# Query norms: in two columns the full high part of the Gram matrix times high parts of x only, read out times x and times the low part of x

## The chip, the cores and the metric

The kernel runs on one NeuronCore of a Trainium2 chip. The metric is the device time of one launch in microseconds. The kernel before takes 480.39 us (median of 3 runs, 479.73 to 480.58).

## What is computed

```
x1  = x + tanh(g0) * attend(layernorm(x), ctx)
      Q = layernorm(x) @ Wq.T + bq ;  K = rmsnorm(ctx) @ Wk.T + bk
      Q = rmsnorm(Q) * qn ;  K = rmsnorm(K) * kn
      attend = softmax(Q @ K.T / 32) @ rmsnorm(ctx)
out = x1 + tanh(g1) * (layernorm(x1) @ W_base.T + b_base + gated low-rank experts)
```

x is 4 batches of 512 tokens by 1024 features, ctx is 4 batches of 64 keys. All is float32. The scores need of Q only its product with K, which goes through a small matrix, and the norm of each of its rows. The norm is taken without forming Q: with z the scaled token and G = Wq^T Wq (rows centred), the square of the norm is z^T G z plus a bias term.

## The kernel before, in words

**High and low parts.** Each float32 operand of a matrix product is split into a high part (rounded to the fast format by ScalarE) and a low part (what is left, VectorE). A product of two such operands is three matmuls: high times high, low times high, high times low.

**Gram matrix.** The `g` stages fill it in two sweeps over banks of PSUM, as 36 blocks of 128x128, each pair (row, column) once, since it is symmetric. `g_out` evicts them: ScalarE writes the high part `gram[:, g, 0, :]`, VectorE the low part `gram[:, g, 1, :]` (L1196); blocks off the diagonal are scaled by 2, which stands for the mirrored block that is not kept. `k_norm` follows early in the second sweep. Then come eight `m` stages (L658 to L660), and then the loop over the four batches.

**Batch loop.** The order of all stages is one list written out by hand (`first`, then `last`), and each engine goes through it in that order and does its own part of each stage; nothing is reordered at run time. For batch b and column j = 0 to 7:

- `y` (b, j): TensorE sums over the blocks of column j, three matmuls each (L673 to L675), into one of three banks. Columns 0 to 7 have 1, 2, 3, 5, 5, 6, 7 and 7 blocks. VectorE's "dot" (L1340) reads the bank, adds a bias and multiplies by z: 128x512 into `sq`, of which there are two that alternate. GpSimd adds each `sq` to `sq_sum` (L1560). A dot waits until the sum has taken the `sq` two before; y (b, j) waits for the dot of three columns before.
- After y (b, 0): `tops` (L702, then L1354) of the batch before, and `mr`. After y (b, 1): `norms` (TensorE L694 adds `sq_sum` over partitions, VectorE L1348, GpSimd a root L1532), `fn_split` (VectorE L1380, two inputs in SBUF), `weights` (VectorE L1513, ScalarE four exponentials), all of the batch before.
- At j = 2: `z` (VectorE L1236) and `zh` (ScalarE) for the batch after, `shares` (VectorE L1360, L1366, L1367, L1369, which makes `px`) and `fn_low` (VectorE L1385) of the batch before. At j = 3: s, `scores`, and `pt`, the transposition of `px` (TensorE L516). In batches 0 and 1 most columns have an `x_stat` too (VectorE L1221, L1224).
- After y (b, 4) to y (b, 7) one `attend` each (TensorE L715, L716 in two halves, each in one of two banks; VectorE L1440 empties them). The next `attend` waits until the bank of its half is empty. It stands in VectorE's order behind `z`.
- In batch 3 VectorE has `stat` at j = 2 (L1160 on), the scaling of `bb` (L1447) at j = 3 and splits of the base weights (L1413) from j = 3 on.

After the loop come the heads and the base product, 8 pairs of token tiles (L736 to L778).

Of the kernel before, what the change touches and what calls it, by code (L numbers as in the profile page):

```python
# [5 lines left out]
P = 128  # L6
# [37 lines left out]
def build(nc, x, xt, ctx, ctxt, wq, wk, wb, hd, bt, vec, fn_w, b_base, scal, out):  # L44
# [9 lines left out]
    B = 4  # L54
# [15 lines left out]
    with ExitStack() as stack:  # L70
# [126 lines left out]
        a21 = at("a21", [P, KH, P], F32, r_a21)  # L197
        csum = at("csum", [P, S_ALL], F32, r_a21)
# [56 lines left out]

        def block_no(row, col):
            return BLOCKS.index((min(row, col), max(row, col)))
# [26 lines left out]
         v_xaggr, v_xvar, v_z, v_zl, v_wq, v_gl, v_ml, v_wb, v_dot, v_top, v_nb, v_rec, v_pxh, v_px, v_fnvar, v_fnw, v_fn,  # L284
         v_wt, v_wl, v_h3, v_hw, v_bb, v_bt, v_neg, v_s3, v_low, v_hg, v_nmax, v_g, v_mm, v_ev) = (
            sem(f"v_{n}") for n in ("ct", "ctxvar", "kw", "small", "stat", "aggr", "var", "kr", "kfull", "kt", "cs", "kb",
# [58 lines left out]
        for p in range(NP):  # L345
# [8 lines left out]
            for i, (n, z, *_) in enumerate(products(p)):  # L354
                if all(z != z_ for _, z_, *_ in products(p)[i + 1:]):
# [22 lines left out]
        for b in range(B):  # L378
            for j in range(FB):
# [23 lines left out]
                if b > 0:  # L403
                    first += {0: [("tops", b - 1)], 1: [("norms", b - 1), ("fn_split", b - 1), ("weights", b - 1)], 2: [("shares", b - 1), ("fn_low", b - 1)],
# [72 lines left out]
        def qsums(b, f):  # L477
            return b * (FB - 1) + f
# [26 lines left out]
        def tensor(pe):  # L505
# [27 lines left out]
            for stage, *i in stages:  # L533
# [90 lines left out]
                elif stage == "g":  # L624
                    sweep, f = i
                    blocks = [w[f][:, :].rearrange("p (c d) -> p c d", d=P) for w in (wqh, wql)]
                    for left, right in ((0, 0), (0, 1), (1, 0)):
                        if sweep == left == 0:
                            pe.wait_ge(*((v_wq, f + 1) if right else (a_wq, f + 1)))
                        for n_bank, pieces in SWEEPS[sweep]:  # L630
# [10 lines left out]
                            if f == FB - 1 and left == 1:  # L641
                                done.then_inc(p_g, 1)
                elif stage == "m":
# [5 lines left out]
                    if r < 2:  # L649
                        engine, count = ring.empty(r)  # L650
# [11 lines left out]
                elif stage == "y":  # L662
# [7 lines left out]
                    pe.wait_ge(v_zl, 4 * b + max(ROWS[j]) // CK + 1)  # L670
                    for r in ROWS[j]:
                        g = block_no(r, j)
                        pe.matmul(acc[:, :], gram[:, g, 0, :], xth[b % 2][:, r, :], start=r == ROWS[j][0], stop=False)  # L673
                        pe.matmul(acc[:, :], gram[:, g, 1, :], xth[b % 2][:, r, :], start=False, stop=False)  # L674
                        done = pe.matmul(acc[:, :], gram[:, g, 0, :], xtl[b % 2][:, r, :], start=False, stop=r == ROWS[j][-1])  # L675
# [13 lines left out]
                elif stage == "norms":  # L689
                    b, = i  # L690
                    acc = ring_open((stage, b), "dve")
                    pe.wait_ge(g_qsum, qsums(b, FB - 1))
# [48 lines left out]
                elif stage == "prod":  # L741
# [3 lines left out]
                    if opens and p == 0:  # L745
                        pe.wait_ge(*{"A": (v_dot, NQ - 2), "B": (v_dot, NQ - 1), "C": (v_first, 4), "D": (v_dot, NQ)}[n_bank])
# [34 lines left out]
        def sync(sp):  # L781
# [42 lines left out]
            for stage, *i in stages:  # L824
# [6 lines left out]
                elif stage == "load_xt":  # L831
# [7 lines left out]
                    else:  # L839
                        sp.wait_ge(p_y, nq(b - 2, FB - 1) + 1)  # L840
                        sp.wait_ge(v_dot, nq(b - 2, FB - 1) + 1)
# [22 lines left out]
                elif stage == "w_load":  # L864
                    op, = i
                    if op in ("B11", "B21", "B12"):
                        sp.wait_ge(p_y, nq(B - 2, FB - 1) + 1)
                        sp.wait_ge(v_dot, nq(B - 2, FB - 1) + 1)
                    elif op in ("B22", "T1", "T2", "T4"):
                        sp.wait_ge(p_y, NQ)  # L870
                        sp.wait_ge(v_dot, NQ)
# [65 lines left out]
        def scalar(act):  # L937
# [13 lines left out]
            for stage, *i in stages:  # L951
# [12 lines left out]
                elif stage == "rsb":  # L964
                    act.wait_ge(p_ring, ring.full((stage,)))
                    act.activation(rsb[:, :], bank[T_BANKS[ring.number[stage,] % 2]][:, 0:S_ALL], ACT.Copy).then_inc(ring_sem["act"], 1)
                elif stage == "tanh":
# [17 lines left out]
                elif stage == "g_out":  # L985
# [3 lines left out]
                    for n, (n_bank, pieces) in enumerate(SWEEPS[sweep]):  # L989
                        act.wait_ge(p_g, n + 1 + sweep * len(SWEEPS[0]))  # L990
                        for row, cols, off in pieces:
                            for c, col in enumerate(cols):
                                done = act.activation(gram[:, block_no(row, col), 0, :],
                                                      bank[n_bank][:, (off + c) * P:(off + c + 1) * P],
                                                      ACT.Copy, scale=1.0 if col == row else 2.0)
# [152 lines left out]
        def vector(dve):  # L1148
# [20 lines left out]
            for stage, *i in stages:  # L1169
# [19 lines left out]
                elif stage == "g_out":  # L1189
                    sweep, = i  # L1190
                    for n, (n_bank, pieces) in enumerate(SWEEPS[sweep]):
                        dve.wait_ge(a_gh, n + 1 + sweep * len(SWEEPS[0]))
                        for row, cols, off in pieces:
                            for c, col in enumerate(cols):
# [3 lines left out]
                                    scalar=1.0 if col == row else 2.0, in1=gram[:, g, 0, :].bitcast(F32),  # L1198
                                    op0=ALU.mult, op1=ALU.subtract)
                        done.then_inc(v_gl, 1)  # L1200
                elif stage == "m_out":
# [130 lines left out]
                elif stage == "y":  # L1332
# [3 lines left out]
                    if n >= 2 and j < 2:  # L1336
                        dve.wait_ge(g_qsum, qsums(b - 1, FB - 2 + j))
                    elif n >= 2:
                        dve.wait_ge(g_qsum, qsums(b, max(1, j - 2)))
# [308 lines left out]
```

## Time and profile before

| | |
|---|---|
| profiled execution | 478.68 us |
| its span, first to last instruction | 476.7 us |
| runs | 479.73, 480.39, 480.58 us |
| TensorE matmul busy | 471.1 us, 99% of the span, 2482 instructions |
| VectorE busy | 353.9 us, 74%, 735 instructions |
| ScalarE busy | 172.4 us, 36%, 347 instructions |
| GpSimd busy | 121.1 us, 25%, 110 instructions |
| DMA engines, mean busy | 48% of 16 |
| granted TensorE clock | 0.998 |

Busy is the time that an engine's records cover. The matmul records overlap, and their ends are modelled, so busy TensorE time is not a measure of what a matmul costs; the distance between two starts is. A record's length on VectorE, too, is a little more than its distance to the next one.

### The profile page before, as it was taken

What the parts mean: (1) busy time and instruction counts of PE and PEld (TensorE: products, weight loads), DVE (VectorE), ACT (ScalarE), POOL (GpSimd) and SP (SyncE); (2) the same over time, 40 slices, a digit from 0 to 9 for tenths busy, and PEclk for the clock granted to TensorE, in tenths of its full rate; (3) what the DMA queues carried; (4) which work ended last, traced back from release to release, by engine and by line L of the source; (5) the groups of instructions that cost most, each with busy time, mean ns of one, the idle gap of its engine ahead of it and who ended that gap; (6) DMA issues with size and microseconds to landing.
All of it is one profiled execution on the core that took longest, in us unless ns stands there. A gap on an engine that the chain in (4) does not pass through costs nothing.

```text
span 476.7 us, 6939 instructions
## 1 busy us (share of the span) xinstructions
PE 471.1 (99%) x2482; PEld 401.3 (84%) x2482; DVE 353.9 (74%) x735; ACT 172.4 (36%) x347; POOL 121.1 (25%) x110
## 2 busy tenths in 40 slices
PE   8999999999999999999999999999999999999997
PEld 6888999998887888888898888888888887888885
DVE  1379896597888967869978888868677678877732
ACT  3795541341214304217326625332241521414300
POOL 1021511003353343345242406031220402305000
PEclk9999999999999999999999999999999999999999
DMA  8995219948676369466579640221405013050202
GB/s 267 411 411 197 84 58 409 382 167 294 196 240 242 134 237 289 187 244 237 183 267 420 280 141 35 78 100 46 133 0 178 0 63 114 1 177 1 89 1 88
DMA packets 22545, 84.39 MB, mean 177 GB/s; under 512 B 2672, under 2 KB 4720, under 8 KB 19696
## 3 DMA queue, kind: packets, MB, share of 16 engines
q1 hardware_dynamic: 22368, 83.94, 48.0%
q8 instruction: 20, 0.33, 0.3%
q14 instruction: 13, 0.11, 0.1%
q10 hardware_dynamic: 144, 0.02, 0.0%
HBM read 61.93 MB, written 22.02 MB: 176 GB/s over the span
## 4 chain that ended last, share of the span: by engine, by line
PE 91%; DMA 6%; DVE 1%; issue 1%; SPq 1%; POOL 0%; DVEq 0%
PE bank L637 11%; PE bank L758 11%; PE bank L762 10%; PE bank L760 10%; PE bank L673 6%; PE bank L675 6%; PE bank L674 6%; PE bank L736 4%; PE bank L516 3%; PE bank L601 2%; DMA out_dram<-xs 2%; DMA xz<-xt_dram 2%; PE bank L659 2%; PE bank L658 2%; PE bank L660 2%; PE bank L738 2%
## 5 line engine op out<-in xcount | busy, mean ns | idle before, releaser
L1532 POOL TENSOR_TENSOR small<-small,tiny 128x1 f32<-128x1 f32 (+2 forms) x25 | 22.7, 907 | 163.1 <-DVE small L1165 138.4
L1506 DVE SCALAR_TENSOR_TENSOR xs<-bank,tiny,xs 128x512 f32<-128x512 f32 x60 | 43.2, 748 | 21.0 <-PE bank L762 15.0
L673 PE MATMUL bank<-xth,gram 128*128 128x512 f32 x144 | 57.3, 398 | 0.0
L675 PE MATMUL bank<-xtl,gram 128*128 128x512 f32 x144 | 56.3, 391 | 0.0
L674 PE MATMUL bank<-xth,gram 128*128 128x512 f32 x144 | 56.1, 390 | 0.0
L1560 POOL TENSOR_TENSOR sq_sum<-sq_sum,sq 128x512 f32<-128x512 f32 x24 | 32.0, 1335 | 59.0 <-DVE sq L1340 59.0
L758 PE MATMUL bank<-wh_B,zh 128*128 128x512 f32 x116 | 47.0, 405 | 0.0
L758 PE MATMUL bank<-wh_T,zh 128*128 128x512 f32 x112 | 45.9, 410 | 0.0
L762 PE MATMUL bank<-wh_B,zl 128*128 128x512 f32 x116 | 45.6, 393 | 0.0
L760 PE MATMUL bank<-wl_B,zh 128*128 128x512 f32 x116 | 45.4, 391 | 0.0
L762 PE MATMUL bank<-wh_T,zl 128*128 128x512 f32 x112 | 44.1, 393 | 0.0
L760 PE MATMUL bank<-wl_T,zh 128*128 128x512 f32 x112 | 44.0, 392 | 0.0
L1593 POOL TENSOR_TENSOR xs<-xs,bb 128x1024 f32<-128x1024 f32 x16 | 39.3, 2460 | 10.4 <-ACT zn L1017 7.8
L1340 DVE SCALAR_TENSOR_TENSOR sq<-bank,gsm,xz 128x512 f32<-128x512 f32 x32 | 23.8, 745 | 14.8 <-PE bank L675 13.3
L974 ACT ACTIVATE xth<-xz 128x1024 fp32r<-128x1024 f32 x16 | 17.0, 1062 | 42.2 <-DVE xz L1236 42.2
L675 PEld LDWEIGHTS bank<-xtl,gram 128*128 128x128 f32 x144 | 27.0, 188 | 5.8
L674 PEld LDWEIGHTS bank<-xth,gram 128*128 128x128 f32 x144 | 27.1, 188 | 5.2
L673 PEld LDWEIGHTS bank<-xth,gram 128*128 128x128 f32 x144 | 27.1, 188 | 5.2
L736 PE MATMUL bank<-hw,zh 128*128 128x276 f32 x128 | 31.1, 334 | 0.0
L738 PE MATMUL bank<-hw,zl 128*128 128x138 f32 x128 | 29.0, 227 | 0.0
L1017 ACT ACTIVATE zn<-xs,small 128x1024 f32<-128x1024 f32 x16 | 19.8, 1240 | 23.1 <-POOL small L1585 23.1
L1042 ACT ACTIVATE zh<-zr 128x512 fp32r<-128x512 f32 x28 | 17.4, 633 | 23.9 <-DVE zr L1276 9.8
(200 smaller groups left out, 1117.8 us busy)
## 6 DMA issues: line engine op xcount, KB each, us to landing
xst<-x_dram SPq DMA_DIRECT2D x16, 512.0 KB, 4.3
xz<-xt_dram SPq DMA_DIRECT2D x16, 512.0 KB, 7.7
out_dram<-xs SPq DMA_DIRECT2D x14, 512.0 KB, 3.7
xa<-x_dram SPq DMA_DIRECT2D x12, 512.0 KB, 3.3
x<-xa SPq DMA_DIRECT2D x12, 512.0 KB, 2.8
xs<-x SPq DMA_DIRECT2D x12, 512.0 KB, 3.9
wq_raw<-wq_dram SPq DMA_DIRECT2D x8, 512.0 KB, 14.7
t_raw_T<-wb_dram SPq DMA_DIRECT2D x4, 1024.0 KB, 16.6
```

The source lines that it names most:

```text
L637: done = pe.matmul(dst, blocks[left][:, row, :], blocks[right][:, cols.start:cols.stop:cols.step, :], start=n == f == left == right == 0, ...
L673: pe.matmul(acc[:, :], gram[:, g, 0, :], xth[b % 2][:, r, :], start=r == ROWS[j][0], stop=False)
L674: pe.matmul(acc[:, :], gram[:, g, 1, :], xth[b % 2][:, r, :], start=False, stop=False)
L675: done = pe.matmul(acc[:, :], gram[:, g, 0, :], xtl[b % 2][:, r, :], start=False, stop=r == ROWS[j][-1])
L736: pe.matmul(acc[:, 0:2 * HEAD], zh[z][:, k, :], hw[w][:, k, :], start=n == k == 0, stop=False, skip_group_check=True)
L738: done = pe.matmul(acc[:, 0:HEAD], zl[z][:, k, :], hw[w][:, k, 0:HEAD], start=False, stop=n == 1 and k == KH - 1, skip_group_check=True)
L758: pe.matmul(acc[:, :], zh[z][:, k, :], wh[op][:, k, :], start=opens and k == 0, stop=False, skip_group_check=True)
L760: pe.matmul(acc[:, :], zh[z][:, k, :], wl[op][:, k, :], start=False, stop=False, skip_group_check=True)
L762: done = pe.matmul(acc[:, :], zl[z][:, k, :], wh[op][:, k, :], start=False, stop=k == KH - 1, skip_group_check=True)
L1506: dve.scalar_tensor_tensor(out=xs[slot][:, half(h)], in0=bank[C_BANK[n_bank]][:, :], scalar=tg[:, 1:2], in1=xs[slot][:, half(h)], op0=ALU. ...
L1560: pool.tensor_tensor(sq_sum[:, :], addend[:, :], sq[j % 2][:, :], ALU.add).then_inc(g_qsum, 1)
L1593: pool.tensor_tensor(xs[slot][:, :], xs[slot][:, :], bb[:, :], ALU.add).then_inc(g_x1, 1)
```

## The change

In columns 0 and 1 the two blocks (0, 1) and (1, 0) are both used, unscaled, and the products are taken with the high part of z alone: high times high and low times high. The missing high times low is recovered at the reading, since the matrix is symmetric: the bank is multiplied by z in one pass and by the low part of z in a second one. The mirrored high block comes from one transposition (stage `gt`); its low part is folded into block (0, 1) by doubling that one.

```diff
+        PURE = 2
+        MIRROR = {pair: n for n, pair in enumerate((r, c) for r in range(PURE) for c in range(r))}
+        gram_t = at("gram_t", [P, len(MIRROR), P], F32R, r_a21)
...
+        ND = FB + PURE
+        def factor(row, col):
+            return 1.0 if row == col or max(row, col) < PURE else 2.0
+        def column(n):
+            return (n if n < FB else (2, 0, 1, 3, 4, 5, 6, 7)[n % FB])
+        def dots(n):
+            return n // FB * ND + sum(1 + (column(n // FB * FB + i) < PURE) for i in range(n % FB))
...
-                 ("g", 1, 2), ("k_norm",), ("x_stat", 3), ("g", 1, 3), ...
+                 ("g", 1, 2), ("k_norm",), ("gt",), ("x_stat", 3), ("g", 1, 3), ...
...
-                    first += {0: [("tops", b - 1)], 1: [("norms", b - 1), ("fn_split", b - 1), ("weights", b - 1)], 2: [("shares", b - 1), ("fn_low", b - 1)],
+                    first += {0: [("tops", b - 1), ("norms", b - 1), ("weights", b - 1), ("fn_split", b - 1)], 1: [("shares", b - 1)], 2: [("fn_low", b - 1)],
                               3: [("load_fn", b)]}.get(j, [])
...
+        def taken(d):
+            return qsums(d // ND, max(1, d % ND))
...  (TensorE)
+                elif stage == "gt":
+                    acc = ring_open((stage,), "act")
+                    pe.wait_ge(a_gh, len(SWEEPS[0]))
+                    for row, col in MIRROR:
+                        n = MIRROR[row, col]
+                        done = pe.transpose(acc[:, n * P:(n + 1) * P], gram[:, block_no(row, col), 0, :].bitcast(F32), ident[:, :])
+                    done.then_inc(p_ring, 1)
...
-                        pe.wait_ge(v_dot, n - 2)
+                        pe.wait_ge(v_dot, dots(n - 2))
+                    j = column(n)
+                    rows = range(PURE) if j < PURE else ROWS[j]
...
+                    for r in rows:
+                        g, opens, closes = block_no(r, j), r == rows[0], r == rows[-1]
+                        if j < r < PURE:
+                            done = pe.matmul(acc[:, :], gram_t[:, MIRROR[r, j], :], xth[b % 2][:, r, :], start=opens, stop=closes)
+                            continue
+                        pe.matmul(acc[:, :], gram[:, g, 0, :], xth[b % 2][:, r, :], start=opens, stop=False)
+                        done = pe.matmul(acc[:, :], gram[:, g, 1, :], xth[b % 2][:, r, :], start=False, stop=closes and j < PURE)
+                        if j >= PURE:
+                            done = pe.matmul(acc[:, :], gram[:, g, 0, :], xtl[b % 2][:, r, :], start=False, stop=closes)
...  (ScalarE)
+                elif stage == "gt":
+                    act.wait_ge(p_ring, ring.full((stage,)))
+                    act.activation(gram_t[:, :, :], ..., ACT.Copy).then_inc(ring_sem["act"], 1)
...  (VectorE, g_out of the first sweep)
+                    if sweep == 0:
+                        dve.wait_ge(v_gd, len(MIRROR))
+                        for row, col in MIRROR:
+                            part = gram[:, block_no(row, col), 1, :]
+                            done = dve.tensor_scalar(part, part.bitcast(F32), 2.0, None, ALU.mult)
+                        done.then_inc(v_gd, 1)
...  (VectorE, y)
+                    acc, j = bank[Y_BANKS[n % 3]], column(n)
+                    for d in entries(n):
+                        if d >= 2:
+                            dve.wait_ge(g_qsum, taken(d - 2))
+                        if d == entries(n)[0]:
+                            dve.scalar_tensor_tensor(out=sq[d % 2][:, :], in0=acc[:, :], scalar=wb2[:, j:j + 1],
+                                                     in1=xz[b % 2][:, j, :], op0=ALU.add, op1=ALU.mult).then_inc(v_dot, 1)
+                        else:
+                            dve.tensor_tensor(sq[d % 2][:, :], acc[:, :], xtl[b % 2][:, j, :].bitcast(F32), ALU.mult).then_inc(v_dot, 1)
...  (GpSimd, y)
+                    for d in entries(nq(b, j)):
+                        n = d % ND
+                        if n == 0:
+                            continue
+                        pool.wait_ge(v_dot, d + 1)
+                        if n > 1:
+                            pool.wait_ge(g_qsum, qsums(b, n - 1))
+                        elif b > 0:
+                            pool.wait_ge(p_ring, ring.full(("norms", b - 1)))
+                        addend = sq[(d - 1) % 2] if n == 1 else sq_sum
+                        pool.tensor_tensor(sq_sum[:, :], addend[:, :], sq[d % 2][:, :], ALU.add).then_inc(g_qsum, 1)
```

In batches 1 to 3 the order of columns becomes 2, 0, 1, 3 and on; in batch 0 it stays. A batch has ten dots and nine sums in place of eight and seven.

## Rows read from the trace of the kernel before

**Rows 1.** Waits of TensorE, whole run: line, releaser, us, times, longest.

```profile
PE bank L516 <- DVE px L1369: 0.2, 1, 0.2
```

**Rows 2.** Timeline of TensorE, batches 0 to 3: start us, us, line.

```profile
119.21 0.39 PE L673 MATMUL bank<-xth,gram 128*128 128x512 f32 x1
...
136.67 0.40 PE L675 MATMUL bank<-xtl,gram 128*128 128x512 f32 x1
...
136.90 1.00 PE L702 MATMUL bank<-ident,st_sb 128*128 128x64 f32 x8
...
139.56 0.95 PE L694 MATMUL bank<-tiny,sq_sum 128*128 128x2 f32 x8
...
158.79 0.40 PE L715 MATMUL bank<-fnh,pt 128*128 128x512 f32 x1
...
205.88 0.39 PE L673 MATMUL bank<-xth,gram 128*128 128x512 f32 x1
...
228.39 0.40 PE L715 MATMUL bank<-fnh,pt 128*128 128x512 f32 x1
```

**Rows 3.** Timeline of VectorE, batch 1; in brackets idle time and releaser.

```profile
136.41 0.75 DVE L1340 SCALAR_TENSOR_TENSOR sq<-bank,gsm,xz 128x512 f32<-128x512 f32 x1 [1.39 <-PE bank L675]
...
137.08 1.28 DVE L1221 BATCH_NORM_STATS2 small<-xst 128x6 f32<-128x512 f32 x2
...
138.52 0.71 DVE L1340 SCALAR_TENSOR_TENSOR sq<-bank,gsm,xz 128x512 f32<-128x512 f32 x1
...
140.55 0.22 DVE L1348 TENSOR_SCALAR small<-bank,tiny 128x4 f32<-128x4 f32 x1
...
140.69 2.35 DVE L1380 SCALAR_TENSOR_TENSOR fn_raw<-fn_raw,small,fnw 128x1024 f32<-128x1024 f32 x1
...
144.02 0.17 DVE L1513 SCALAR_TENSOR_TENSOR small<-small 128x4 f32<-128x4 f32 x1 [0.99 <-POOL small L1532]
...
147.48 1.22 DVE L1236 TENSOR_TENSOR xz<-xz,bank 128x1024 f32<-128x1024 f32 x1 [1.16 <-DMA xz<-xt_dram]
...
149.62 1.22 DVE L1385 TENSOR_TENSOR fnl<-fn_raw,fnh 128x1024 fp32r<-128x1024 f32 x1
...
157.11 1.40 DVE L1440 SCALAR_TENSOR_TENSOR xa<-bank,rt,xa 128x512 f32<-128x512 f32 x2
```

**Rows 4.** Timeline of VectorE, one dot that waited for GpSimd.

```profile
112.62 0.75 DVE L1340 SCALAR_TENSOR_TENSOR sq<-bank,gsm,xz 128x512 f32<-128x512 f32 x1 [1.47 <-POOL sq_sum L1560]
```

**Rows 5.** Timeline of GpSimd: sums of squares and roots.

```profile
111.23 1.28 POOL L1560 TENSOR_TENSOR sq_sum<-sq,sq 128x512 f32<-128x512 f32 x1 [11.44 <-DVE sq L1340]
...
141.91 2.00 POOL L1532 TENSOR_TENSOR small<-small,tiny 128x4 f32<-128x4 f32 x1
...
222.38 2.29 POOL L1560 TENSOR_TENSOR sq_sum<-sq_sum,sq 128x512 f32<-128x512 f32 x1
...
246.20 1.02 POOL L1532 TENSOR_TENSOR small<-small,tiny 128x4 f32<-128x4 f32 x1 [1.87 <-DVE small L1348]
```

**Rows 6.** Timeline of VectorE in batch 3.

```profile
213.54 1.28 DVE L1160 BATCH_NORM_STATS2 small<-xs 128x6 f32<-128x512 f32 x2
...
216.09 1.33 DVE L1366 TENSOR_SCALAR rt<-small,tiny 128x4 f32<-128x4 f32 x1
...
219.12 0.75 DVE L1447 TENSOR_SCALAR bb<-bb,tiny 128x1024 f32<-128x1024 f32 x1
...
221.46 4.29 DVE L1413 TENSOR_TENSOR wl_B<-wr_B,wh_B 128x1024 fp32r<-128x1024 f32 x2 [0.93 <-ACT wh_B L1116]
...
226.33 1.39 DVE L1440 SCALAR_TENSOR_TENSOR xa<-bank,rt,xa 128x512 f32<-128x512 f32 x2
```

**Rows 7.** All instructions of line 1380: duration ns least, median, most.

```profile
L1380 DVE SCALAR_TENSOR_TENSOR fn_raw<-fn_raw,small,fnw x4: 1275/2345/2346, 140.7 to 260.8; 128x1024 f32<-128x1024 f32 x4
```

**Rows 8.** Timeline of ScalarE and VectorE between the two Gram sweeps.

```profile
78.94 2.01 ACT L1123 ACTIVATE t_high_T<-t_raw_T 128x1024 fp32r<-128x1024 f32 x2 [13.83 <-DMA T_low<-t_low_T]
...
58.83 0.42 DVE L1303 TENSOR_TENSOR kr<-bank,rsb 128x256 f32<-128x256 f32 x1 [1.89 <-PE bank L608]
```

More of the change, by code:

```diff
@@ L254, in build, with entries @@
         assert len([b for b in SWEPT[0] if b[1] <= 4]) == 10 and len(SWEPT[1]) >= 16
+        ND = FB + PURE
[5 more added lines that the diff above has]
+            return n // FB * ND + sum(1 + (column(n // FB * FB + i) < PURE) for i in range(n % FB))
+        def entries(f):
+            return range(dots(f), dots(f + 1))
         def block_no(row, col):
@@ L668, in tensor @@
                     elif n >= 3:
-                        pe.wait_ge(v_dot, n - 2)
[L670 to L675, printed above, removed]
+                        pe.wait_ge(v_dot, dots(n - 2))
+                    j = column(n)
+                    rows = range(PURE) if j < PURE else ROWS[j]
+                    pe.wait_ge(v_zl, 4 * b + max(rows) // CK + 1)
+                    if n == 0:
+                        pe.wait_ge(v_gd, len(MIRROR) + 1)
+                        pe.wait_ge(ring_sem["act"], ring.empty(ring.number["gt",])[1])
+                    for r in rows:
[7 more added lines that the diff above has]
+                            done = pe.matmul(acc[:, :], gram[:, g, 0, :], xtl[b % 2][:, r, :], start=False, stop=closes)
                     done.then_inc(p_y, 1)
@@ L840, in sync @@
                         sp.wait_ge(p_y, nq(b - 2, FB - 1) + 1)
-                        sp.wait_ge(v_dot, nq(b - 2, FB - 1) + 1)
+                        sp.wait_ge(v_dot, dots(nq(b - 2, FB - 1) + 1))
                     load_xt(b)
@@ L994, in scalar @@
                                                       bank[n_bank][:, (off + c) * P:(off + c + 1) * P],
-                                                      ACT.Copy, scale=1.0 if col == row else 2.0)
+                                                      ACT.Copy, scale=factor(row, col))
                         done.then_inc(a_gh, 1)
@@ L1197, in vector @@
                                     out=gram[:, g, 1, :], in0=bank[n_bank][:, (off + c) * P:(off + c + 1) * P],
-                                    scalar=1.0 if col == row else 2.0, in1=gram[:, g, 0, :].bitcast(F32),
+                                    scalar=factor(row, col), in1=gram[:, g, 0, :].bitcast(F32),
                                     op0=ALU.mult, op1=ALU.subtract)
+                                if row != col and factor(row, col) == 1.0:
+                                    done.then_inc(v_gd, 1)
                         done.then_inc(v_gl, 1)
+                    if sweep == 0:
[3 more added lines that the diff above has]
+                            done = dve.tensor_scalar(part, part.bitcast(F32), 2.0, None, ALU.mult)
+                        done.then_inc(v_gd, 1)
                 elif stage == "m_out":
@@ L1335, in vector @@
                     dve.wait_ge(p_y, n + 1)
[L1336 to L1339, printed above, removed]
-                    dve.scalar_tensor_tensor(out=sq[n % 2][:, :], in0=bank[Y_BANKS[n % 3]][:, :], scalar=wb2[:, j:j + 1],
-                                             in1=xz[b % 2][:, j, :], op0=ALU.add, op1=ALU.mult).then_inc(v_dot, 1)
+                    acc, j = bank[Y_BANKS[n % 3]], column(n)
[7 more added lines that the diff above has]
+                            dve.tensor_tensor(sq[d % 2][:, :], acc[:, :], xtl[b % 2][:, j, :].bitcast(F32), ALU.mult).then_inc(v_dot, 1)
                 elif stage == "norms":
```

28 lines of the change are left out of this document (12 added, 16 removed), and 4 rows, old and new, of tables (first, ring_sem).

## The prediction

> **What bounds the kernel now.** The waits of TensorE come first. In a span of 476.7 us the only one in the batch loop is 0.2 us, for `px` from VectorE [rows 1]. TensorE issues back to back there, and a matmul taken out shortens the run as long as the others keep up. Its price is not the 0.39 us of its record but the step between two starts: from 119.21 to 136.67 lie the y matmuls of columns 4 to 7 (25 blocks, 75 matmuls) and of column 0 of the next batch (3), 77 steps in 17.46 us, 0.227 each [rows 2].
>
> The timeline of VectorE comes second, at the places where TensorE needs it. In batch 1 the second `attend` starts at 158.79 [rows 2]. It needs the first half of the first one emptied; L1440 starts at 157.11 and does two halves in 1.40, so that half is free at about 157.85 [rows 3]. With 0.13 for a signal, TensorE has 0.8 us to spare. In batch 3 the same pair is 228.39 [rows 2] and 226.33 [rows 6], 1.2 us to spare. From 149.62 to 157.11 no row of VectorE has idle time in front of it: it is the second bound, close behind.
>
> **TensorE's part.** Columns 0 and 1 have 3 blocks, 9 matmuls; now 2 + 1 + 2 + 2 = 7. Two less in four batches: 8 x 0.227 = 1.82 us off. Added is one transposition of 128x128. `tops` and `mr`, twelve small matmuls, take 139.56 - 136.90 - 6 x 0.227 = 1.30, 0.11 each [rows 2], so 0.11 and at most one record of 0.48 if nothing overlaps. ScalarE copies it inside 13.83 us in which it waits for a DMA, and the doubling of a low block fits into VectorE's 1.89 us [rows 8]; if that cover were gone it would be some 0.3 us on engines that are not the bound there. So -1.71 us if nothing else gave way.
>
> **VectorE's and GpSimd's part.** A dot takes 0.67 us (136.41 to 137.08), an `x_stat` 1.44 (to 138.52), `z` 1.13, `shares` the 1.0 that remains between 147.48 and 149.62 [rows 3]. No row has the second dot, a bank times one SBUF tile. It lies between 0.6, half of a 1024-wide pass of 1.275 less overlap [rows 7], and the 0.75 of a first dot's whole record [rows 4]; I take 0.63. A sum on GpSimd starts 0.83 us after its dot, takes 1.28, and the dot that needs it follows 0.11 later (111.23 + 1.28 = 112.51, dot at 112.62) [rows 4, 5]. This wait becomes exposed: `sq` has two tiles, so the third dot of a batch waits for its first sum, and the second and third are now both of column 0 with no TensorE work between. It costs 0.83 + 1.28 + 0.11 - 0.67 = 1.55 us. Behind it in VectorE's queue stand `shares`, two more dots, `z`, `fn_low` and the emptying of `attend`.
>
> **Batch 1, step by step**, in times of the trace; TensorE is 0.34 early by then.
> - y (1, 0) has 9 matmuls now: 136.22 - 0.34 + 2.05 = 137.93. `tops` 0.87, then `norms` at once, 138.80. L1348 starts 0.99 after it (139.56 to 140.55) [rows 2, 3]: 139.79. The root follows its 0.22 and a signal, and takes the 1.02 of 246.20, not the 2.00 of 141.91 [rows 5]: 141.11. `weights` waits for it with nothing between: 141.22.
> - `fn_split` next. Three of four took 2.35, the least 1.275 [rows 7]; the one at 140.69 lay over a sum on GpSimd. Now GpSimd is idle: it ends 142.54, 1.07 saved.
> - First dot of column 0 to 143.21, wait, second dot 144.76 to 145.39.
> - `shares`: L1366 comes 0.83 after the second dot's start, with the second sum. Batch 3 has that meeting: 1.33 us for four elements a partition [rows 6]. So `shares` takes 2.15: 147.54.
> - Two dots of column 1, 148.84; `x_stat` 150.28; `z` 151.41 (the DMA that held it until 147.48 is there).
> - `fn_low` starts at 151.41 and not 149.62, so `attend` is emptied 7.49 later, at 158.90 and not 157.11 [rows 3]. Half free 159.64, signal 159.77.
> - TensorE wants it at 158.79 - 0.34 - 0.45 = 158.00 and stalls 1.75 us.
>
> The 1.33 of 216.09, the 4.29 for two splits at 221.46 [rows 6] and the 2.29 of a sum at 222.38 [rows 5] say that some VectorE work and a sum on GpSimd exclude each other; dots are not touched. The Trainium skill ("SBUF — State Buffer", Who interferes with whom) has the cause: GpSimd's only port pair is VectorE's second one, the first to start holds it for its whole instruction, and an instruction with two SBUF inputs or in a fast two-port mode needs it. By that rule the eight added sums, on an engine that is busy a quarter of the time, cost VectorE time wherever they meet `shares`, `fn_low`, the scaling of `bb` or a split; by busy time alone they would be free. The trace agrees, with 1.33 us.
>
> **Batch 2.** The same without two `x_stat` (3.1 us less), with `fn_low` and one low split over a sum (up to 1.6 more): 0 to 1 us, I take 0.35. TensorE starts batch 3 at -0.34 - 0.45 + 1.75 - 0.45 + 0.35 = +0.85.
>
> **Batch 3.** The same steps from 205.88 + 0.85: y (3, 0) to 208.78, L1348 210.64, `weights` 212.07, `fn_split` to 213.39, second dot 215.61 to 216.24, `shares` 218.39. Only now come `stat` (216.09 - 0.21 - 0.67 - 213.54 = 1.67, which before stood in front of `shares`) and two dots: `fn_low` could start at 221.36, where it started at 219.12 - 1.14 = 217.98. Two sums follow the two dots. `fn_low` stands 0.9 for one and ends at 223.4; `bb` stands 1.3 for the next and ends at 225.4, before at 219.8. The bias on GpSimd needs `bb`, so its meeting with the splits moves along, and `attend` is emptied 226.33 - 219.79 = 6.54 later, at 231.95. Half free and told 232.8. TensorE wants it at 228.39 + 0.85 - 0.45 = 228.8: 4.0 us, of which some 0.3 falls already at the first `attend`, for `fn_low`. Without the two blocks it would be 1.8.
>
> **Sum.** -1.71 + 1.75 + 0.35 + 4.0 = +4.4 us: 478.68 + 4.4 = 483.1 for the profiled execution, which is 1.7 under the median of the runs shown; on that median 480.39 + 4.4 = 484.8. After the loop both kernels are alike.
>
> **Rivals.**
> - A, as above, 482.0 (no blocks in batch 3, a shorter second dot) to 487.0 (1 us in batch 2, 0.6 each at the third and fourth `attend` of batch 3). For it: spare times of 0.8 and 1.2 us against VectorE 1.8 and 5.6 us later. 0.60.
> - B, all waits hidden, faster: -1.71, 478.7. `px` is no longer behind a DMA, VectorE has 1.47 and 0.99 us of idle time to give [rows 3, 4], and `fn_split` gains 1.07. Against it: it needs L1440 of batch 1 at its old time, and each of these is already in the ledger. 0.15.
> - C, even: stalls of 1.0 in batch 1 and 0.8 in batch 3, 480.5, if the exposed wait overlaps with the one for the root. Against it: the one stands before `fn_split` and the other behind. 0.13.
> - D, worse: VectorE's lateness in batch 3 reaches the third and fourth `attend` and the heads, whose splits stand behind them. From 1 us more on VectorE than in the ledger TensorE loses it again at each: +6.6 or more, 487 and over. 0.12.
>
> **Chances.** A measurement here tells 0.2%, 0.96 us, from no change. Faster by more: B and a little of C, 0.17. Within: 0.11. Slower: A, D and the rest of C, 0.72. The range of 8 in 10 leaves out the greater part of B and the tail of D: 479.4 to 488.6.
>
> **What would show it.** Right: y matmuls of 144, 144, 132 and 4, 424 in all; TensorE waits for the emptying of `attend`, 1.8 us in batch 1 and 4 in batch 3; the third dot of every batch waits about 1.5 for a sum; `fn_split` at 1.28 and the root at 1.02; the instruction of L1366 at 1.3 in batches 1 to 3. Wrong: no waits of TensorE in the batch loop, or waits at `norms` or `pt` in place of `attend`; a second dot over 0.75; `fn_low` and `bb` of batch 3 at their old lengths.

## The result, and the profile after

The changed kernel takes 483.12 us (median of 5 runs, 482.87 to 484.33), the one before 479.73 (5 runs, 477.35 to 480.58). The ratio is 1.010, with a 95% interval of 1.0081 to 1.0119: slower by about 1%, clear of the noise. The forecast was +4.4 us on the time of before, the medians say +3.4, the ratio +4.8. The profiled execution took 482.87 us, its span is 481.0, against 478.68 and 476.7.

From the page of the profile, the busy times and two of the lines of y matmuls (L714 and L715 have 144 records each, L717 132, and the mirrored block four more):

```profile
PE 471.7 (98%) x2475; PEld 400.7 (83%) x2475; DVE 362.5 (75%) x744; ACT 171.6 (36%) x348; POOL 129.4 (27%) x118
...
L714 PE MATMUL bank<-xth,gram 128*128 128x512 f32 x144 | 57.8, 402 | 0.0
...
L717 PE MATMUL bank<-xtl,gram 128*128 128x512 f32 x132 | 52.0, 394 | 0.0
```

The matmuls are gone as counted. TensorE's busy time is what it was (471.7 us, before 471.1), though the span is 4.3 us longer. The waits of TensorE (line, releaser, us in all, times, longest) say where it stands; `attend` is L757 now:

```profile
PE bank L757 <- DVE xa L1497: 3.6, 2, 3.0
...
PE bank L757 <- issue: 0.7, 1, 0.7
```

The wait for `px` of [rows 1] is gone, and in its place stand 3.6 us for `xa`, the emptying of `attend`, and 0.7 for which the view names no releaser. In the timeline of TensorE these are, in order: first, second and third `attend` of batch 1, then of batch 3 (start us, us):

```profile
153.12 0.47 PE L757 MATMUL bank<-fnh,pt 128*128 128x512 f32 x1 [0.75 <-issue]
...
158.98 0.50 PE L757 MATMUL bank<-fnh,pt 128*128 128x512 f32 x1 [0.62 <-DVE xa L1497]
...
164.98 0.40 PE L757 MATMUL bank<-fnh,pt 128*128 128x512 f32 x1
...
222.81 0.47 PE L757 MATMUL bank<-fnh,pt 128*128 128x512 f32 x1
...
231.55 0.51 PE L757 MATMUL bank<-fnh,pt 128*128 128x512 f32 x1 [3.02 <-DVE xa L1497]
...
239.62 0.40 PE L757 MATMUL bank<-fnh,pt 128*128 128x512 f32 x1
```

Set against the same instructions of before (158.79 and 228.39 of [rows 2], and 153.76, 164.49, 222.90 and 234.56, which stand at the same places of its timeline), TensorE is 0.64 us early at 153.12, 0.19 late at 158.98, 0.49 at 164.98, 0.09 early at 222.81, 3.16 late at 231.55 and 5.06 late at 239.62. It stays about 5.05 late until near 400 and is 4.3 late from there on, because at 401 the profiled execution of before lost 0.75 to a load of `xs`, which the changed one didn't.

The 0.7 without a releaser is a wait that the forecast doesn't have. The last y matmul in front of the first `attend` of batch 1 starts at 151.98, 1.55 us earlier than its like of before (153.53), and `attend` starts at 153.12, 0.91 later than it would have behind a step of 0.227. In the program it waits there for `fn_low` (over at 151.91) and for ScalarE's copy of `pt`. In ScalarE's order this copy stands behind `zh`, which needs VectorE's `z`. ScalarE's timeline, `pt` of before, then `zh` and `pt` of the changed kernel:

```profile
150.52 0.60 ACT L1086 ACTIVATE pt<-bank 128x512 fp32r<-128x512 f32 x1
```

```profile
150.81 1.06 ACT L1020 ACTIVATE xth<-xz 128x1024 fp32r<-128x1024 f32 x1 [7.21 <-DVE xz L1290]
...
152.44 0.59 ACT L1132 ACTIVATE pt<-bank 128x512 fp32r<-128x512 f32 x1
```

The copy is over at 153.03, and `attend` starts 0.09 later. `z` itself starts at 149.60, where it started at 147.48 [rows 3]: `shares` and the two dots of column 1 stand in front of it now.

VectorE in batch 1 (idle time and releaser in brackets), answering to [rows 3]: `weights`, `fn_split`, first and second dot of column 0, `rt` in `shares`, `fn_low`, the emptying of the first `attend` (first half):

```profile
140.79 0.16 DVE L1570 SCALAR_TENSOR_TENSOR small<-small 128x4 f32<-128x4 f32 x1 [1.21 <-POOL small L1589]
...
140.90 1.28 DVE L1437 SCALAR_TENSOR_TENSOR fn_raw<-fn_raw,small,fnw 128x1024 f32<-128x1024 f32 x1
...
142.10 0.74 DVE L1395 SCALAR_TENSOR_TENSOR sq<-bank,gsm,xz 128x512 f32<-128x512 f32 x1
...
144.25 0.69 DVE L1398 TENSOR_TENSOR sq<-bank,xtl 128x512 f32<-128x512 f32 x1 [1.40 <-POOL sq_sum L1621]
...
145.06 1.27 DVE L1423 TENSOR_SCALAR rt<-small,tiny 128x4 f32<-128x4 f32 x1
...
150.69 1.22 DVE L1442 TENSOR_TENSOR fnl<-fn_raw,fnh 128x1024 fp32r<-128x1024 f32 x1
...
158.18 0.75 DVE L1497 SCALAR_TENSOR_TENSOR xa<-bank,rt,xa 128x512 f32<-128x512 f32 x1
```

`fn_split` takes 1.28 for 2.35. The second dot of column 0 waits 1.40 for the sum. L1423, the old L1366, takes 1.27. `fn_low` starts at 150.69 (forecast 151.41), and the emptying 7.49 us later, at 158.18 (158.90). VectorE in batch 3, answering to [rows 6]: `rt`, the first half of `stat`, `fn_low`, `bb`, two splits of base weights, the emptying (first half):

```profile
215.82 1.28 DVE L1423 TENSOR_SCALAR rt<-small,tiny 128x4 f32<-128x4 f32 x1
...
217.67 0.69 DVE L1206 BATCH_NORM_STATS2 small<-xs 128x6 f32<-128x512 f32 x1
...
220.61 2.00 DVE L1442 TENSOR_TENSOR fnl<-fn_raw,fnh 128x1024 fp32r<-128x1024 f32 x1
...
222.54 1.78 DVE L1504 TENSOR_SCALAR bb<-bb,tiny 128x1024 f32<-128x1024 f32 x1
...
224.90 5.28 DVE L1470 TENSOR_TENSOR wl_B<-wr_B,wh_B 128x1024 fp32r<-128x1024 f32 x2
...
230.76 0.74 DVE L1497 SCALAR_TENSOR_TENSOR xa<-bank,rt,xa 128x512 f32<-128x512 f32 x1
```

`fn_low` takes 2.00 where [rows 3] has 1.22, and `bb` 1.78 where [rows 6] has 0.75, and the two splits 5.28 where they had 4.29. GpSimd, a root and the two sums behind `stat`, answering to [rows 5]:

```profile
139.66 1.02 POOL L1589 TENSOR_TENSOR small<-small,tiny 128x4 f32<-128x4 f32 x1 [1.91 <-DVE small L1405]
...
220.24 3.53 POOL L1621 TENSOR_TENSOR sq_sum<-sq_sum,sq 128x512 f32<-128x512 f32 x2
```

The root takes 1.02, and the two sums 3.53 in place of 2.6: `fn_low` runs until 222.61, and the second sum, 1.3 us long, ends at 223.77, so it stood still until `fn_low` was nearly over.

What the forecast doesn't have is the clock. Busy time by stretch, of PE, PEld, DVE, ACT and POOL; after the count of POOL comes the granted clock, as a share of 2.4 GHz, then the DMA's share and GB/s:

```profile
228.50:231.50 3.00, 0.03 (x1) 0.00 (x0) 3.00 (x4) 0.00 (x0) 1.18 (x2) 1.00 0.00 0
231.50:233.00 1.50, 1.45 (x7) 0.96 (x8) 1.50 (x2) 0.00 (x0) 0.69 (x1) 1.00 0.00 0
233.00:236.40 3.40, 3.40 (x12) 2.73 (x11) 3.37 (x6) 0.60 (x1) 0.00 (x0) 0.50 0.41 159
236.40:239.60 3.20, 3.20 (x15) 2.64 (x14) 3.17 (x7) 1.25 (x1) 2.00 (x3) 1.00 0.96 296
```

TensorE issues nothing from 228.5 to 231.5. It starts again at the full clock, and from 233.0 its clock is at the lower level, 1.2 GHz, for 3.4 us; a y matmul that took 0.227 from start to start takes 0.43 there (233.82, 234.25, 234.68 in the timeline). The 6.17 us from one `attend` to the next become 8.07. Of the 1.90 more, 0.3 are lost ahead of 233.0, at the second half of the same `attend`, as in batch 1 (0.19 late at 158.98, 0.49 at 164.98, with the clock at full speed there); the other 1.6 are the clock's.

### The profile page after: what moved, and what is told of

Same layout as the page of the kernel before. It is cut to its first block, busy times and chain, and to the rows that moved or that the text cites. A ratio compares the mean times of both kernels' runs of the same rounds, so it can differ in the third digit from the quotient of the medians.

```text
span 481.0 us, 6954 instructions
## 1 busy us (share of the span) xinstructions
PE 471.7 (98%) x2475; PEld 400.7 (83%) x2475; DVE 362.5 (75%) x744; ACT 171.6 (36%) x348; POOL 129.4 (27%) x118
## 4 chain that ended last, share of the span: by engine, by line
PE 88%; DVE 6%; issue 3%; POOL 2%; DMA 1%; ACT 0%; DVEq 0%; POOLq 0%; ACTq 0%
PE bank L800 11%; PE bank L804 11%; PE bank L802 11%; PE bank L663 10%; PE bank L714 5%; PE bank L715 5%; PE bank L778 5%; PE bank L717 5%; PE bank L542 3%; PE bank L627 2%; PE bank L780 2%; PE bank L692 2%; PE bank L691 2%; PE bank L693 2%; PE bank L818 2%
## 5 line engine op out<-in xcount | busy, mean ns | idle before, releaser
L1589 POOL TENSOR_TENSOR small<-small,tiny 128x1 f32<-128x1 f32 (+2 forms) x25 | 19.7, 789 | 169.1 <-DVE small L1211 137.2
L714 PE MATMUL bank<-xth,gram 128*128 128x512 f32 x144 | 57.8, 402 | 0.0
L1621 POOL TENSOR_TENSOR sq_sum<-sq_sum,sq 128x512 f32<-128x512 f32 x32 | 43.1, 1348 | 51.6 <-DVE sq L1395 48.5
L715 PE MATMUL bank<-xth,gram 128*128 128x512 f32 x144 | 56.7, 394 | 0.0
L717 PE MATMUL bank<-xtl,gram 128*128 128x512 f32 x132 | 52.0, 394 | 0.0
L715 PEld LDWEIGHTS bank<-xth,gram 128*128 128x128 f32 x144 | 27.5, 191 | 5.5
L714 PEld LDWEIGHTS bank<-xth,gram 128*128 128x128 f32 x144 | 27.5, 191 | 5.5
L717 PEld LDWEIGHTS bank<-xtl,gram 128*128 128x128 f32 x132 | 25.1, 190 | 5.5
L804 PEld LDWEIGHTS bank<-wh_B,zl 128*128 128x128 f32 x116 | 21.8, 188 | 5.0
```

Of the source, the lines that this page charges most:

```text
L715: done = pe.matmul(acc[:, :], gram[:, g, 1, :], xth[b % 2][:, r, :], start=False, stop=closes and j < PURE)
L804: done = pe.matmul(acc[:, :], zl[z][:, k, :], wh[op][:, k, :], start=False, stop=k == KH - 1, skip_group_check=True)
L1621: pool.tensor_tensor(sq_sum[:, :], addend[:, :], sq[d % 2][:, :], ALU.add).then_inc(g_qsum, 1)
```

## The experiments

Each is timed in five rounds beside runs of the kernel before on its own chip, and the ratio is to those. "us won" and "lost" are ratio times 479 where nothing else is said.

**Two matmuls less and nothing else**, in the kernel before. What is left out is the high times low product of column 1.

```diff
-                        pe.matmul(acc[:, :], gram[:, g, 1, :], xth[b % 2][:, r, :], start=False, stop=False)
-                        done = pe.matmul(acc[:, :], gram[:, g, 0, :], xtl[b % 2][:, r, :], start=False, stop=r == ROWS[j][-1])
+                        done = pe.matmul(acc[:, :], gram[:, g, 1, :], xth[b % 2][:, r, :], start=False, stop=j == 1 and r == ROWS[j][-1])
+                        if j != 1:
+                            done = pe.matmul(acc[:, :], gram[:, g, 0, :], xtl[b % 2][:, r, :], start=False, stop=r == ROWS[j][-1])
```

> The kernel before, in which column 1 leaves out its two matmuls of high part times low part of z (two matmuls less per batch, nothing else; the norms miss that product). Theory (a y matmul is worth its step of 0.227 us, TensorE is the bound in the batch loop): 8 x 0.227 = 1.8 us less, ratio 0.996. Rival (TensorE's earlier arrival is lost again in the loop, VectorE being the true bound): between 0 and 0.9 us less, with new waits of TensorE at the emptying of attend, for which it had 0.8 us to spare.

Measured 477.15 us (9 runs) against 479.17, ratio 0.9951 (0.9933 to 0.9969), 2.3 us won, 1.5 to 3.2. The price of 1.8 lies in the interval, and the rival's 0 to 0.9 doesn't. The profiled run, at 480.3 the highest of the nine, lost the gain again in waits of TensorE; the others, 1.5 to 4.2 us lower, have no trace:

```profile
PE bank L516 <- DVE px L1370: 2.1, 2, 1.4
...
PE bank L716 <- DVE xa L1441: 1.3, 1, 1.3
```

**Without the second readings.** The changed kernel, matmuls and order of stages kept.

```diff
-        ND = FB + PURE
+        ND = FB
...
         def dots(n):
-            return n // FB * ND + sum(1 + (column(n // FB * FB + i) < PURE) for i in range(n % FB))
+            return n
```

> The changed kernel without its second readings and their sums (the norms miss the product with the low part of z at the reading); matmuls, transposition and the new order of stages stay. Theory (VectorE is late through the second dots, the exposed wait for the first sum and the sums that block shares, fn_low and bb): all waits of TensorE at attend vanish, 1.7 us less than before (about 478.0), against 3.4 to 4.8 more for the changed kernel. Rival (the new order of stages is what makes VectorE late): at least 1 us slower than before.

Measured 477.66 (12 runs), ratio 0.9975 (0.9959 to 0.9991), 1.2 us won. The sign turns, so the second readings with their sums make the loss, and the new order doesn't. The 1.7 lie in the interval. The profiled run, at 480.64 the highest of the twelve, has one wait at `attend` after all, the fourth of batch 3:

```profile
241.69 0.50 PE L757 MATMUL bank<-fnh,pt 128*128 128x512 f32 x1 [2.27 <-DVE xa L1497]
```

VectorE stood 2.46 us for a load of the head weights ahead of it, and behind it the clock was at the lower level for 3.4 us. The other waits at `attend` are gone, the one for `pt` too.

**The old order of stages and columns** in the changed kernel: the list of stages of before, apart from `gt`, and columns 0, 1, 2 in every batch.

```diff
-                    first += {0: [("tops", b - 1), ("norms", b - 1), ("weights", b - 1), ("fn_split", b - 1)], 1: [("shares", b - 1)], 2: [("fn_low", b - 1)],
+                    first += {0: [("tops", b - 1)], 1: [("norms", b - 1), ("fn_split", b - 1), ("weights", b - 1)], 2: [("shares", b - 1), ("fn_low", b - 1)],
```

> The changed kernel in the old order of stages and columns (norms after y (b, 1), fn_split ahead of weights, shares at j = 2 behind z, columns 0, 1, 2 in every batch). Theory (the reordering repairs more than it costs; without it the third dot waits for a sum that waits for norms, and root and exponentials come later): slower than the changed kernel by 2 us or more, TensorE waiting at pt too. Rival (the reordering is the cause of the loss): 1.7 us less than before.

Measured 487.46 (6 runs: two at 484, four above 487), ratio 1.0146 (1.0116 to 1.0176), 7.0 us lost and 2.2 more than with the new order, though the two intervals just touch. In the profiled run, one of the two at 484, the waits are at `pt`, once in each of three batches:

```profile
PE bank L542 <- DVE px L1426: 5.7, 3, 2.5
```

The reordering is a repair. It moves the trouble from `pt` to `attend` and, by the ratios, makes it smaller. The rival, that the reordering is the loss, is out: the old order is slower than before, not faster.

**A third `sq` tile** in the changed kernel; the mirrored block moves to another free place, and `% 2` becomes `% 3` where `sq` is used.

```diff
-        sq = [at(f"sq{i}", [P, TB], F32, r_sq + i * TB * WORD) for i in range(2)]
+        sq = [at(f"sq{i}", [P, TB], F32, o) for i, o in enumerate((r_sq, r_sq + TB * WORD, r_a21))]
...
-                        if d >= 2:
-                            dve.wait_ge(g_qsum, taken(d - 2))
+                        if d >= 3:
+                            dve.wait_ge(g_qsum, taken(d - 3))
```

> The changed kernel with a third sq tile (the mirrored block moves to another free place), so that the third dot need not wait for the first sum. Theory (sums and VectorE's two-input or fast-mode instructions exclude each other, so the sums that no longer make the dot wait stand in front of L1366 and L1367 in place of that): shares ends only some 0.6 us earlier than in the changed kernel, the whole 1 to 3 us faster than it (3 if the pause of TensorE in batch 3 gets too short to lower the clock), not faster than before. Rival (the wait for the sum alone is the cost): 1.5 us earlier in each batch, no wait of TensorE in batch 1, at most 1.5 in batch 3, and about the time of before or 0.5 less.

Measured 482.81 (6 runs), ratio 1.0069 (1.0044 to 1.0093): 1.5 us better than the changed kernel by the two ratios, whose intervals overlap, and still slower than before. VectorE's timeline in batch 1: `weights`, then `rt` and the last instruction of `shares`, then the next dot:

```profile
141.73 0.16 DVE L1570 SCALAR_TENSOR_TENSOR small<-small 128x4 f32<-128x4 f32 x1 [1.21 <-POOL small L1589]
...
144.51 0.68 DVE L1423 TENSOR_SCALAR rt<-small,tiny 128x4 f32<-128x4 f32 x1
...
145.42 1.46 DVE L1426 TENSOR_TENSOR px<-pexp,px 128x256 fp32r<-128x256 f32 x1
...
146.80 0.74 DVE L1395 SCALAR_TENSOR_TENSOR sq<-bank,gsm,xz 128x512 f32<-128x512 f32 x1
```

The wait of 1.40 is gone from in front of the dot. In its place L1423 takes 0.68 where it has 0.23 alone, and L1426, with both inputs in SBUF, 1.46 where its like takes 0.43 in batch 1 of before. From `weights` to the first dot of column 1 it is 5.07 us, against 146.90 - 140.79 = 6.11: 1.04 won of 1.40, where I had expected 0.6. A part of the wait comes back as sums that stand in front of other work: 0.45 at L1423 and 1.03 at L1426, against 1.04 at L1423 alone in the changed kernel. The rival, that the wait is the whole cost, had asked for the time of before.

**`shares` behind `stat` in batch 3**, in the changed kernel.

```diff
-..., 1: [("shares", b - 1)], 2: [("fn_low", b - 1)],
+..., 1: [("shares", b - 1)] * (b < B - 1), 2: [("shares", b - 1)] * (b == B - 1) + [("fn_low", b - 1)],
```

> The changed kernel, in which batch 3 does shares after stat and y (3, 2) as before the change. Theory (two things made batch 3 dear: 3.0 us of idle TensorE at the second attend, and 3.4 us of half clock that follow it and cost 1.7): px comes 2 us later, so TensorE waits some 2 us at pt and only about 1 at attend; the idle time is about the same in sum but in shorter pieces; if a long idle piece is what lowers the clock, the clock stays and 1.5 us or so is won over the changed kernel; if not, the time is that of the changed kernel within 0.5. Rival (the order of shares and stat is the cause of batch 3's loss): the waits of TensorE in batch 3 vanish, 3 us or more are won.

Measured 482.24 (6 runs), ratio 1.0059 (1.0038 to 1.008), 2.0 us better than the changed kernel, with intervals that lie just apart. Its waits:

```profile
PE bank L542 <- DVE px L1426: 2.5, 1, 2.5
...
PE bank L757 <- DVE xa L1497: 1.0, 2, 0.6
```

The 2.5 at `pt` is in batch 3. At `attend` there are 0.6 in batch 1 and 0.4 at the fourth `attend` of batch 3, besides the 0.7 for `pt` in batch 1. The clock of the profiled run stays at 1.00 through the loop. In sum TensorE stands about as long as in the changed kernel (4.2 us for 4.3), and what is won is near the price of the slow stretch, but VectorE met fewer sums too, so this run alone doesn't separate the two. The next two do.

**A pause for TensorE and nothing else.** In the kernel before, in front of the second `attend` of batch 3; the second version has `v_stat, 2`.

```diff
+                    if t == 9:
+                        pe.wait_ge(v_first, 1)
```

> The kernel before with one more wait on TensorE, in front of the second attend of batch 3, where the changed kernel stood for 3.0 us: it waits for the low part of the first base tile, which by the trace of before comes 2.3 us after TensorE gets there. Nothing else. Theory (a pause costs its own length, and a longer one half clock behind it too): 2.3 us slower than before with the clock at full speed. Rival (the half clock of the changed kernel had nothing to do with its pause): same here, so this run tells only together with the longer pause.

> The same wait, on the statistics of the second tile, 3.5 us after TensorE gets there. Theory: the granted clock falls to half behind the pause for some 3.4 us, so that it costs 3.5 + 1.7 = 5.2 us. Rival (the clock fell by chance or through something else in the changed kernel): 3.5 us, granted clock at full speed in the loop.

The pauses, in TensorE's timeline, short and then long:

```profile
231.91 0.50 PE L717 MATMUL bank<-fnh,pt 128*128 128x512 f32 x1 [2.10 <-DVE zl L1261]
```

```profile
231.42 0.79 PE L717 MATMUL bank<-fnh,pt 128*128 128x512 f32 x1 [3.29 <-DVE small L1162]
```

Short: 481.29 (12 runs) against 478.64, ratio 1.0052 (1.0034 to 1.0071). The runs are of two kinds: seven have a mean granted clock of 1.00 or 0.999 and a median of 480.49, five have 0.996 and a median of 482.15. One stretch of 3.4 us at half clock makes a mean of 0.996 over a span of 480, and the difference is 1.7 us. Long: 483.43 (6 runs), ratio 1.0094 (1.0072 to 1.0115), a mean clock of 0.993 or 0.996 in five of six, and 4.5 us (4.8 by the medians) for a pause of 3.3, as traced. Its stretches after the pause:

```profile
232.00:234.00 2.00, 2.00 (x9) 1.59 (x7) 1.74 (x3) 0.00 (x0) 1.85 (x3) 0.50 1.00 304
234.00:236.00 2.00, 2.00 (x10) 1.64 (x9) 2.00 (x3) 1.56 (x2) 0.00 (x0) 0.85 0.81 284
```

The theory holds with a correction: behind the short pause the clock fell too, in some runs and not in others. The traced one is a run without the fall, so the pauses of the others aren't known. The other traces say the same: the clock was at the lower level for 3.4 us behind a pause of 2.24 at `attend` with a third `sq`, of 2.27 without the second readings and of 2.52 in batch 3 with the old order, and it stayed at 1.00 behind 2.31 in batch 1 of that same trace and behind 2.46 with `shares` behind `stat`. So the experiment with `stat` doesn't show that a shorter pause keeps the clock up.

**`shares` ahead of `z`** in the kernel before.

> The kernel before with shares moved ahead of z at j = 2 in batches 1 to 3, nothing else. Theory: px no longer stands behind the DMA of the next batch, TensorE's wait of 0.2 at pt in batch 1 goes, 0.2 to 0.3 us less, no more than noise. Rival (shares now meets a sum on GpSimd in batches 1 and 2 as well, 1.3 us): TensorE gets a new wait at pt or attend and the kernel is 0.5 to 1 us slower.

Measured 478.88 (12 runs) against 478.90, ratio 0.9989 (0.9976 to 1.0003). Nothing that can be told from no change; the wait for `px` is gone from its trace.

**One reading.** The changed kernel's matmuls with eight dots per batch, in the order of before with `shares` ahead of `z`. The tile that a dot multiplies by, columns 0 and 1 of z, is made z plus its low part once per batch (so the bias is multiplied by that too, one low part more than in the reference):

```diff
+                elif stage == "zz":
+                    b, = i
+                    dve.wait_ge(v_zl, 4 * b + 4)
+                    dve.tensor_tensor(xz[b % 2][:, 0:PURE, :], xz[b % 2][:, 0:PURE, :], xtl[b % 2][:, 0:PURE, :].bitcast(F32),
+                                      ALU.add).then_inc(v_zz, 1)
```

> A version meant to beat both: the changed kernel's matmuls, but one reading of columns 0 and 1, times z plus its low part; that sum is made in place once per batch by one VectorE pass of 1024 elements (1.2 us), for the next batch at j = 7, where VectorE waits 1.4 to 2.5 us for TensorE. Eight dots and seven sums per batch as before, order as before with shares ahead of z. (The bias is multiplied by the same sum, a difference of one low part.) Theory: TensorE's 1.7 us stay won and nothing waits: 1.7 to 2.0 us less than before, about 478. Rival (any further pass on VectorE is paid by TensorE): even with before or slower, with waits of TensorE at attend.

Measured 477.60 (12 runs), ratio 0.9985 (0.9962 to 1.0008). Seven runs lie at 477.0 to 477.7, five at 479.5 to 481.6, three of these with a mean clock of 0.995 or 0.996. The interval holds the 1.7 won as well as nothing. The traces of the first two experiments point to a cause of such upper values; this is VectorE in that with two matmuls less, in batch 3:

```profile
238.57 0.73 DVE L1424 TENSOR_TENSOR hw_raw<-hw_raw,hw_raw 128x552 f32<-128x552 f32 x1 [2.13 <-DMA hw_raw<-hd_dram]
```

VectorE stands 2.13 us for the head weights, and behind it TensorE 1.3 at the last `attend` of batch 3. The load is queued behind a load of x that waits for a store. None of the five upper runs has a trace. So three more kernels have it right behind y (3, 4):

```diff
-                              5: [("zt", 0, "a11"), ("stat", 1), ("load_hd",)],
+                              5: [("zt", 0, "a11"), ("stat", 1)],
...
                 first.append(("y", b, j))
+                if b == B - 1 and j == 4:
+                    first.append(("load_hd",))
```

> The changed kernel with the load of the head weights queued right behind y (3, 4) and not behind a load of x that waits for a store. Theory (the loss in batch 3 is VectorE's chain up to the second attend; the head weights, for which VectorE stood 0.9 us in the changed kernel, come too late for it to matter to TensorE): within 0.7 us of the changed kernel, ratio to before 1.007 to 1.010. Rival (that DMA is a large part of the loss): 1.5 us or more won.

> The version with one reading (z plus its low part) and the same early load of the head weights. In the version without it 7 of 12 runs lay at 477.0 to 477.7 and 5 at 479.5 to 481.6. Theory (the upper ones come from VectorE standing for the head weights, which makes TensorE wait at the last attend, as the traces with two matmuls less and without second readings show, 1.4 and 2.3 us): the upper group goes, median 477.2, ratio 0.9955. Rival (the upper group has another cause): it stays, ratio near 0.9985.

> The kernel before with the same early load of the head weights. Theory (there VectorE is not reached by it: it has no idle time in front of the head weights): no change within 0.2%. Rival (the scatter of before, 477.4 to 481.7, is that DMA too): its upper values go and the median falls by 0.5 us or more.

In the changed kernel it does nothing: 483.42 (6 runs), ratio 1.0097 (1.0074 to 1.012). These six runs fall in line with the clock: 481.81 at a mean of 1.00, 483.01 to 483.44 at 0.996 and 484.23 and 484.62 at 0.993. With one reading it makes the version that beats both: 476.31 (12 runs, 475.99 to 477.19) against 478.52, ratio 0.9952 (0.9934 to 0.9971), 2.3 us won, and no upper group. Its only wait of TensorE over 0.2 us in all is the one at the start, and the pass that makes the sum fits where VectorE stood idle before y's last dot (1.39 us at 136.41 in [rows 3]):

```profile
PE bank L566 <- DVE idle L1222: 1.2, 1, 1.2
```

```profile
135.19 1.23 DVE L1310 TENSOR_TENSOR xz<-xz,xtl 128x1024 f32<-128x1024 f32 x1
```

In the kernel before it gives 478.49 (12 runs) against 478.52, ratio 0.9984 (0.9965 to 1.0003): the median stays, and the highest run is 479.64, against 482.99 of 23 beside it. So the theory was right on the median. Whether the scatter of before is that DMA too stays open: only 6 of the 23 runs beside it lie above 479.64, and none of them has a trace.

## Why the prediction was right

By its own steps (the ledger is the forecast's running sum of what TensorE wins and loses):

- **TensorE's part, -1.71.** Right in the count and the price: two matmuls less alone win 1.5 to 3.2 us, and y matmuls count 144, 144, 132 and 4. Not in the forecast: TensorE came into the loop at 107.27 where before has 107.60, though 0.11 later was forecast. That is chance between executions, for kernels with these same matmuls came there at 107.27 to 108.21. And the wait for `px` in batch 1, 0.31 from step to step, went. The two together make TensorE 0.75 earlier than the forecast has it.
- **The exposed wait, 1.55.** Right. Between the starts of the two dots lie 2.15 us in each of three batches (142.10 to 144.25), forecast 2.22, so the wait is 1.48 in the forecast's terms, 1.40 as idle time between records.
- **The meetings of sums and VectorE's work.** Right in kind and nearly in size: `rt` 1.27 (forecast 1.33) in all of batches 1 to 3, `fn_split` 1.28 for 2.35, `fn_low` 2.00 and `bb` 1.78 in batch 3. A third `sq` shows it from the other side: when the wait goes, a sum stands in front of L1426 too.
- **Batch 1, 1.75.** Near in size and half wrong in kind. TensorE goes from 1.55 early at 151.98 to 0.49 late at 164.98, so it stood for 2.04. Only 1.1 of this is the emptying of `attend`, which came 0.7 earlier than forecast, since `norms` did by 0.4 and the steps behind it were each a little shorter. The other 0.91 is the copy of `pt` on ScalarE behind `zh` and `z`, a path that the forecast doesn't have; it has `z` start 2.8 us later than before, at 150.28, and asks only what stands behind it on VectorE. With what TensorE was early, the end of the batch is 0.49 late, forecast 0.96.
- **Batch 2, 0.35.** About nothing: 0.09 late at the third `attend` from 0.49 before, less the 0.45 won.
- **Batch 3, 4.0.** 0.27 up to and at the first `attend`, 3.25 at the second and 0.29 at its second half, 3.8 in all. The chain on VectorE from the start of y (3, 0) to the emptying was forecast at 25.2 us, and is 230.76 - 205.97 = 24.8.
- **The half clock.** Missing from the sum: 1.6 us behind the pause of batch 3, and 1.7 between runs with and without it when a pause alone is put in. As measured the ledger is -0.33 at the start of the loop, -1.82 for the matmuls, -0.31 for `px`, +2.04, +0.05 and +3.81 for the three batches and +1.61 for the clock, 5.05 in sum, and TensorE was 5.06 late at 239.62. A load of `xs` in the execution of before took 0.75 of this back. That the total forecast was near is in part luck: the three stalls came out 0.2 less than forecast in sum (5.9 for 6.1), and a clock that nobody had in the sum was set off by an early start, by `px` and by that load, 1.5 together.
- **Rivals.** B, all hidden, is out, and would have come true with one reading and the early load: then VectorE has no more dots and sums, and 2.3 us are won. C is out. D's way, lateness at the third and fourth `attend`, isn't there: TensorE has no wait behind the second. That its half clock gave VectorE the time to recover is likely, and was not tried by itself; with `shares` behind `stat`, where the clock stayed up, the fourth `attend` of batch 3 has a wait of 0.4. The reordering as the cause of the loss was in no forecast, and the old order puts it at 2.2 us to the good, at the edge of the noise. But the wait for `pt` on ScalarE is a price of the new order together with the added dots: it puts them in front of `z`.

What stays open: the clock fell behind some pauses of 2.1 to 2.5 us and not behind others, and nothing here says what decides it. Dots without sums, or sums without dots, were not run, so how the loss divides between VectorE's added passes (some 0.6 each) and their meetings with sums is read from the timelines alone. One of the changed kernel's five runs has a mean clock of 1.0 and is not faster than the others. What it lost in place of that has no trace.

## What to carry to other kernels

Before work moves from the engine that bounds the kernel to one that is 75% busy, read how far the second one is ahead at the place where the first waits for it: here 0.8 and 1.2 us, and eight short passes were too many. Follow what depends on the moved work through the other engines' orders too: `z` made a copy on ScalarE late for which TensorE then stood. A sum on GpSimd, which looks free, cost VectorE up to 1.1 us at a `tensor_scalar` or an instruction with two inputs in SBUF that it met; so ask first whether two readings can be one, by changing what is multiplied and not how often. And a pause of the matmul engine of 2 to 3 us can cost 1.6 to 1.7 more than itself, not in every run.

## What the runs showed of the hardware

- The granted clock of TensorE fell to its lower level, 1.2 GHz, for 3.4 us behind a pause of 3.0 us (changed kernel) and 3.3 (the long pause), with TensorE at work without a gap ahead of it and behind it. Behind pauses of 2.24, 2.27 and 2.52 it did so too, behind 2.10, 2.31 and 2.46 it didn't. With the short pause put in, five of twelve runs have the mean clock of such a stretch. The price is 1.6 to 1.7 us each time.
- While a sum of 1.28 us runs on GpSimd, a `tensor_scalar` over four elements a partition takes 1.27 in place of 0.23, and a `tensor_tensor` with both inputs in SBUF 1.46 in place of 0.43; dots, with one input in PSUM, keep their 0.74, and `bn_stats` its 1.28. When both wait in turn, they alternate: two sums 3.53, `fn_low` 2.00, `bb` 1.78.
- A load of 276 KB twice, queued behind one that waits for a store, held VectorE for 2.13 and 2.46 us in two traces, and TensorE behind it for 1.35 and 2.27. With it ahead in the queue, the version with one reading has its highest run at 477.19 in place of 481.59, and the kernel before its median where it was.
